# A fused recurrent tower on one core: TensorE's order rearranged, the recurrence in two blocks, half-height first scores, masks by chunk

## The chip, the cores and the metric

The program runs on one core of one Trainium2 chip. The metric is the device time of one execution in microseconds, median of the runs shown. The core's engines are TensorE (PE), VectorE (DVE), ScalarE (ACT), GpSimd (POOL) and SyncE (SP, which issues DMAs here).

## The reference, cut to what matters

```python
# x: 64 sequences of 128 token ids; table rows (50257 x 256) are quantised by tier
h   = take(quantised_table, x)                     # 64 x 128 x 256
# a layer norm, then block_forward; in its mixer, per sequence and head (8 heads of 64, 16 states):
def step((z, y), (dt, B, C, u)):
    z = (z + dt * (u*B - A*y)) / (1 + dt*dt*A)
    y = y + dt * z
    out = einsum('hpn,n->hp', y, C)
yout = (ys + D_skip * u) * silu(zgate)
x = x + yout @ out_proj.T                          # then an MLP: 256 -> 1024 -> gelu -> 256
# at last a layer norm and an int8-weight linear layer with a residual
```

The step is linear in (z, y), with a 2 x 2 matrix that depends on the head, the state and the time, but not on u. The kernel therefore computes products of these matrices along time, turns them into "keys" and "queries", and gets the outputs of 64 steps at once, as masked scores (keys times queries) times u.

## The kernel before

The program has three parts. Part one streams the embedding table to find its tier maxima and gathers the rows (0 to about 178 us). Part two is a pipeline of turns over 16 groups of 4 sequences (512 tokens a group). Part three quantises the result and multiplies by the int8 weights (the last 55 us or so). The change lies in part two.

In turn g every engine works on three groups: `first` (group g: projections, convolution, the recurrence), `second` (p = g-1: keys, queries, scores, scan output, gate, output projection) and `third` (m = g-2: the MLP and the statistics of the last norm). There are 18 turns, 0 to 17; turns 2 to 15 have all three. Each engine's order within a turn is written out by hand in `pe_turn`, `act_turn`, `dve_turn` and `pool_turn`, and semaphores join them. An engine runs its list strictly in order.

PE's list in a full turn is: `pe_z` of tiles 0 and 1 (p), transposes of the rows of g (L591), `pe_z` 2 and 3 (each waits for DVE's convolution of its tile), `pe_mlp_T` (L1030, waits for ACT's scaled rows, which wait for DVE's `dve_rms`), `pe_small` (L614), then the MLP of m: fc1 tile n (L1048) and fc2 tile n-3 (L1067), interleaved for n = 0 to 10. `pe_u_T` (L888) of p turns u back to tokens, two of four before the last two fc2 tiles, two behind. Then for each half of the heads, hg = 0 and 1: `pe_scores` (L927), a wait for DVE's masks, `pe_scan_out` (L952) in two pairs. Then `pe_u` (L604, four tiles) and `pe_out` (L973).

DVE's list is: quantise, small convolution, `dve_d` (L667), `dve_keys` (L770 to L812, waits for ACT's squares L756), `dve_layer_norm` (L907), `dve_inverse` (L815), `dve_queries`, `dve_h2`, four masks, the statistics of m, skip and gate of tiles 0 and 1, four masks, the statistics of group g+1 (L541), skip and gate of tiles 2 and 3, `dve_mean3` (L1104), `dve_bc`, the convolution of u in three portions (L851) with `dve_rms_rows` and `dve_x2` (L981) between, `dve_rms` (12 tiny dependent operations on 128x4, L997 to L1013), `dve_bk` (L733, two) and `dve_max3`.

POOL's list is: `pool_residual` (two operations on 128x1024, L1077 and L1081), 32 steps of the recurrence, `pool_norm_factors` of g+1 (waits for DVE's statistics), `pool_rstd3` (L1112 and L1114; it waits for `dve_mean3`), 32 more steps. A step is a multiplication (L747) and an addition (L749), each on 128x32 elements (2 rows of 16 lanes), and each waits for the one before. A lane stands for one chunk of 64 tokens of one sequence and head half, so 64 steps cover all. The next turn's squares on ACT (L756) need all of them.

Score matmuls have 128 keys for both chunks (ch = 0, 1) of a sequence. For chunk 0 the keys 64 to 127 are masked away by `causal`. Each mask (L938) reads a whole PSUM bank, 128x512. Scores use the banks `sbk` and `tb`; `sbk` is also where fc2 accumulates.

Of the kernel before, what the change touches and what calls it, by code (L numbers as in the profile page):

```python
# [26 lines left out]
ACT = mybir.ActivationFunctionType  # L27
# [20 lines left out]
CL = LEN // CH  # L48
SC = G * CH
# [36 lines left out]
def build(nc, a, out):  # L86
    with ExitStack() as ctx:
# [335 lines left out]
        Gs = sb("Gs", [P, CL + 1, 2, LANES])  # L423
        stp = sb("stp", [P, 2, LANES])
# [53 lines left out]
        rec = signal("rec", 2 * CL)  # L478
# [15 lines left out]
        m_ready = signal("m_ready", HG * 4)  # L494
# [241 lines left out]
        def pool_recurrence(pool, g, steps):  # L736

            if steps[0] == 0:
                if since(g):

                    pool.wait_ge(kq.sem, kq.at(g - 1))
                    pool.wait_ge(k_ready.sem, k_ready.at(g - 1))
                pool.wait_ge(x_ready.sem, x_ready.at(g))
            for t in steps:
                if t:
                    pool.wait_ge(rec.sem, rec.at(g, 2 * t))
                pool.tensor_tensor(stp[:], Gs[:, t, ::-1, :], X2[:, t, :, :], ALU.mult).then_inc(rec.sem, 1)  # L747
                pool.wait_ge(rec.sem, rec.at(g, 2 * t + 1))
                pool.tensor_tensor(Gs[:, t + 1, :, :], Gs[:, t, :, :], stp[:], ALU.add).then_inc(rec.sem, 1)  # L749

        def act_squares(act, g):
# [4 lines left out]
            act.activation(sq.rearrange("p (t a l) -> p t a l", t=CL, a=2), Gs[:, 1:, :, :], ACT.Square, scale=DOWN40) \  # L756
                .then_inc(sq_ready.sem, 1)

        def first(ap):

            return ap.rearrange("p t (s c) -> p c s t", c=CH)[:, 0]

        def second(ap):
            return ap.rearrange("p t (s c) -> p c s t", c=CH)[:, 1]

        def dve_keys(dve, g):
# [8 lines left out]
            dve.tensor_tensor(Kf[:, :, 0:CL], first(bk[:]), first(Gs[:, 0:CL, 1, :]), ALU.mult).then_inc(k_ready.sem, 1)  # L775
            dve.tensor_tensor(Kf[:, :, 2 * CL:3 * CL], second(bk[:]), second(Gs[:, 0:CL, 1, :]), ALU.mult) \
# [28 lines left out]
            t1 = sq[:, 0:2 * SC * CL].rearrange("p (a s t) -> p a s t", a=2, s=SC)  # L805
            bcast = lambda i: ends[:, i, :].unsqueeze(2).to_broadcast([P, SC, CL])
            dve.tensor_tensor(t1[:, 0], first(Gs[:, 0:CL, 1, :]), bcast(2), ALU.mult).then_inc(kq.sem, 1)
            dve.tensor_tensor(t1[:, 1], first(Gs[:, 0:CL, 0, :]), bcast(3), ALU.mult).then_inc(kq.sem, 1)
# [3 lines left out]
            dve.tensor_tensor(Kf[:, :, CL:2 * CL], first(bk[:]), t1[:, 0], ALU.mult).then_inc(k_ready.sem, 1)  # L812
# [12 lines left out]
        def pe_u(pe, g):  # L825
            for f in range(UT):
# [104 lines left out]
        def dve_mask(dve, g, hg, hh):  # L931
# [4 lines left out]
            elif since(g):  # L936
                dve.wait_ge(y_mm.sem, y_mm.at(g - 1))
            dve.tensor_tensor(MT[hh][:], score_bank[hh][:, :].rearrange("p (j t) -> p j t", j=G),  # L938
                              causal[:].rearrange("p c t -> p (c t)").unsqueeze(1).to_broadcast([P, G, LEN]),
                              ALU.mult).then_inc(m_ready.sem, 1)  # L940

        def pe_scan_out(pe, g, hg, pair):
            if hg == 0 and pair == 0:

                pe.wait_ge(z_ready.sem, z_ready.at(g))
                if since(g):
                    pe.wait_ge(gelu.sem, gelu.at(g - 1))
            pe.wait_ge(m_ready.sem, m_ready.at(g, 4 * hg + 2 * pair + 2))
# [193 lines left out]
        def pe_turn(pe):  # L1142
            def turn(g, first, second, third, nxt):
# [504 lines left out]
```

## Time and profile before

| | us |
|---|---|
| median of 3 runs | 1468.62 |
| lowest to highest | 1467.59 to 1469.27 |
| the profiled execution's own time | 1464.07 |
| its span, first to last instruction | 1462.2 |
| PE matmul busy | 1184.4 |
| DVE busy | 1160.4 |
| POOL busy | 819.6 |
| ACT busy | 757.9 |

Busy times are sums over the whole span. The span contains a streaming part in which PE does little, so they don't tell what limits a turn; for that the timeline of one turn must be read. The granted clock of TensorE has two levels here, 1.00 (2.4 GHz) and 0.50 (1.2 GHz); its mean is 0.915.

### The profile page before, as it was taken

To read this page: it belongs to the slowest core of one execution; us is meant where nothing else is said; L and a number is where in the kernel's file an instruction comes from. 1 tells how busy PE (TensorE), PEld (TensorE's weight loads), DVE (VectorE), ACT (ScalarE), POOL (GpSimd) and SP (SyncE) were. 2 spreads that over 40 slices of the span, in tenths; PEclk is the share of its full clock that TensorE was granted. 3 is DMA by queue.
4 is the path that set the end of the run, shared out by engine and by line. 5 is a ranking of instruction groups with operands and counts; after the bars stand their busy time and mean duration, and the time that the engine had idled before them with its cause. 6 is when DMAs were issued, how large, how long until landed. Compare 5 with 4: busy or idle time off the path is not lost. (4 is left out here: it accounts for less than half of the span.)

```text
span 1462.2 us, 25531 instructions
## 1 busy us (share of the span) xinstructions
PE 1184.4 (81%) x7199; PEld 814.6 (56%) x7206; DVE 1160.4 (79%) x2087; ACT 757.9 (52%) x1108; POOL 819.6 (56%) x2326
## 2 busy tenths in 40 slices
PE   0694043498989898989898989899999999898767
PEld 0352021357575756676767666666666675757444
DVE  4899933678888889888888989888888978878268
ACT  4667352354637373828273737473736555451247
POOL 7860027574757566575757575757575757560100
PEclk9999996599989899989899989998989989999889
DMA  9999400000001010101000000000000000000015
GB/s 367 408 407 425 160 23 16 12 19 16 23 10 31 1 32 3 30 6 26 10 22 16 16 16 16 16 16 16 16 16 16 16 16 16 18 17 1 0 42 188
DMA packets 62068, 92.22 MB, mean 63 GB/s; under 512 B 9101, under 2 KB 55010, under 8 KB 57554
## 3 DMA queue, kind: packets, MB, share of 16 engines
q1 hardware_dynamic: 58386, 82.10, 15.8%
q0 software_dynamic: 3072, 8.39, 1.5%
q10 hardware_dynamic: 576, 1.31, 0.2%
q8 instruction: 16, 0.26, 0.1%
q14 instruction: 18, 0.15, 0.0%
HBM read 81.29 MB, written 10.49 MB: 63 GB/s over the span
## 5 line engine op out<-in xcount | busy, mean ns | idle before, releaser
L747 POOL TENSOR_TENSOR stp<-Gs,X 128x32 f32<-128x32 f32 x1024 | 290.4, 284 | 263.1 <-ACT X L722 152.9
L749 POOL TENSOR_TENSOR Gs<-Gs,stp 128x32 f32<-128x32 f32 x1024 | 286.6, 280 | 80.3
L1048 PE MATMUL bank<-mT,w_fc 128*128 128x512 f32 x512 | 236.3, 599 | 7.9 <-ACT mT L1036 7.9
L604 PE MATMUL bank<-xT,w_in 128*128 128x512 f32 x512 | 235.8, 610 | 8.0 <-DVE uT L851 8.0
L1067 PE MATMUL bank<-w_fc,gl 128*128 128x256 f32 x1024 | 236.5, 379 | 0.0
L1067 PEld LDWEIGHTS bank<-w_fc,gl 128*128 128x128 f32 x1024 | 193.4, 190 | 59.8 <-issue 37.5
L837 ACT ACTIVATE uT<-bank,cols 128x512 f32<-128x512 f32 x64 | 49.5, 778 | 276.6 <-PE bank L604 276.6
L604 PEld LDWEIGHTS bank<-xT,w_in 128*128 128x128 f32 x512 | 97.7, 196 | 117.6 <-issue 107.1
L1048 PEld LDWEIGHTS bank<-mT,w_fc 128*128 128x128 f32 x512 | 95.7, 192 | 100.1 <-issue 94.7
L952 PE MATMUL bank<-MT,utok 128*64 128x128 f32 x1024 | 112.1, 408 | 45.5 <-DVE MT L938 45.4
L851 DVE SCALAR_TENSOR_TENSOR uT<-bank,cols,uT 128x500 f32<-128x500 f32 (+1 forms) x192 | 135.1, 736 | 3.0 <-ACT uT L837 0.7
L339 DVE TENSOR_TENSOR peak<-ring,peak 128x1536 f32<-128x1536 f32 (+2 forms) x67 | 115.3, 1722 | 19.4 <-ACT ring L242 18.0
L952 PEld LDWEIGHTS bank<-MT,utok 128*64 128x64 f32 x1024 | 101.1, 219 | 50.6 <-DVE MT L938 45.7
L938 DVE TENSOR_TENSOR MT<-bank,causal 128x512 f32<-128x512 f32 x128 | 79.5, 683 | 58.4 <-PE bank L927 58.4
L1058 ACT ACTIVATE gl<-bank,cols 128x512 f32<-128x512 f32 x128 | 84.6, 684 | 74.8 <-PE bank L1067 66.1
L242 ACT ACTIVATE ring<-ring 128x3072 f32<-128x3072 f32 (+3 forms) x35 | 90.8, 2598 | 51.0 <-DMA ring<-in_table 51.0
L973 PE MATMUL bank<-w_out,sz 128*128 128x256 f32 x512 | 113.7, 380 | 0.3 <-DVE sz L964 0.3
L973 PEld LDWEIGHTS bank<-w_out,sz 128*128 128x128 f32 x512 | 97.1, 190 | 20.9 <-issue 7.5
L815 DVE RECIPROCAL rm<-rm 128x1024 f32<-128x1024 f32 x16 | 104.7, 6542 | 0.0
L927 PE MATMUL bank<-Qf,Kf 32*128 32x64 f32 x2048 | 81.4, 319 | 21.0 <-ACT utok L897 11.2
L280 PE MATMUL bank<-ts,hot 4*128 4x256 f32 x128 | 60.4, 648 | 40.1 <-ACT hot L253 39.0
L927 PEld LDWEIGHTS bank<-Qf,Kf 32*128 32x128 f32 x2048 | 76.6, 230 | 29.2 <-issue 29.2
(171 smaller groups left out, 1899.8 us busy)
## 6 DMA issues: line engine op xcount, KB each, us to landing
ring<-in_table SPq DMA_DIRECT2D x32, 1536.0 KB, 20.9
d_rep<-d_rows SPq DMA_DIRECT2D x128, 64.0 KB, 2.7
out<-res SPq DMA_DIRECT2D x16, 512.0 KB, 2.9
b_rep<-bc_rows SPq DMA_DIRECT2D x128, 32.0 KB, 1.8
c_rep<-bc_rows SPq DMA_DIRECT2D x128, 32.0 KB, 1.8
w_fc<-in_w_fc SPq DMA_DIRECT2D x2, 1024.0 KB, 8.8
w_in<-in_w_in ACTq DMA_DIRECT2D x1, 1088.0 KB, 5.2
h<-in_table,ids POOLq DMA_INDIRECT x64, 9.8
```

What stands on the lines that cost most here:

```text
L242: act.activation(ring[n % RING][0:np_, 0:nr, :], ring[n % RING][0:np_, 0:nr, :], ACT.Abs) \
L339: return dve.tensor_tensor(acc, ring[t][0:np_, r0:r0 + nr, :], acc, ALU.max)
L604: last = pe.matmul(dst, w_in[:, k, c0:c1], xT[:, k, :], start=(k == 0), stop=(k == KD - 1))
L747: pool.tensor_tensor(stp[:], Gs[:, t, ::-1, :], X2[:, t, :, :], ALU.mult).then_inc(rec.sem, 1)
L749: pool.tensor_tensor(Gs[:, t + 1, :, :], Gs[:, t, :, :], stp[:], ALU.add).then_inc(rec.sem, 1)
L815: dve.reciprocal(rm[:], rm[:]).then_inc(inverted.sem, 1)
L851: dve.scalar_tensor_tensor(acc[:, :, i:], ps[:, :, 0:LEN - i], c("u_tap", f * TAPS + TAPS - 1 - i), acc[:, :, i:], ALU.mult, ALU.add).then ...
L927: last = pe.matmul(score_bank[hh][:, t:t + CL], Kf[own, hg * G + j, ch * CL:ch * CL + P], Qf[own, hg, t:t + CL], start=True, stop=True)
L952: last = pe.matmul(pj[head // 2][64 * (head % 2):64 * (head % 2) + 64, j * LEN:(j + 1) * LEN], utok[:, j, head * HP:(head + 1) * HP], MT[h ...
L973: last = pe.matmul(sbk[n][:, (j % 2) * D:(j % 2 + 1) * D], sz[:, f, j * LEN:(j + 1) * LEN], w_out[:, f, :], start=(f == 0), stop=(f == UT ...
L1048: last = pe.matmul(pj[n % 4][:, :], w_fc1[:, k, n * P:(n + 1) * P], mT[:, k, :], start=(k == 0), stop=(k == KD - 1))
L1067: last = pe.matmul(sbk[j // 2][:, (j % 2) * D:(j % 2 + 1) * D], gl[n % LEAD][:, j * LEN:(j + 1) * LEN], w_fc2[:, n, :], start=(n == 0 and ...
```

## The change

1. **Recurrence in two blocks.** The 64 steps of a lane become two blocks of 32 (`RB = 2`, `BL = 32`) that run side by side. `Gs` gets a block dimension. Block 1 starts from a unit state. A step's operations now cover 128x64 elements, and there are 32 steps. Before them POOL writes the unit state (one operation on 128x32), and after them `pool_join` rotates and scales all 33 states of block 1 by the end of block 0: two operations on 128x1056 and two on 128x528, all on POOL. Everything that reads `Gs` gets one more dimension.
2. **PE's order.** All four `pe_u_T` and the scores of hg = 0 move into the end of the MLP loop, the scores ahead of the last fc2 tile. `pe_u` is split: tiles 0 and 1 run between the scores of hg = 1 and their scan output, tiles 2 and 3 behind it. Scores move to the banks `tb[0], tb[1], pj[2], pj[3]`, so that they need not wait for `dve_h2`.
3. **Scores and masks.** Chunk 0 multiplies by 64 keys only. The lower 64 rows of its part of `MT` are zeroed once at the start (four memsets). A mask becomes two operations, 64x256 and 128x256: 16 a turn for 8.
4. **DVE's order.** `dve_layer_norm` moves from ahead of the inverse to behind `dve_mean3`; the row statistics of g+1 move ahead of the masks; `dve_h2` goes behind the first masks; skip is split from gate; statistics and mean of m go behind the last gate; `dve_bc` goes behind the first convolution portion.

```diff
@@ the recurrence on POOL
+                pool.tensor_tensor(Gs[:, 1, 0, :, :], unit[:], unit[:], ALU.mult).then_inc(rec.sem, 1)
+            X4 = X2[:].rearrange("p (b t) a l -> p b t a l", b=RB)
             for t in steps:
-                if t:
-                    pool.wait_ge(rec.sem, rec.at(g, 2 * t))
-                pool.tensor_tensor(stp[:], Gs[:, t, ::-1, :], X2[:, t, :, :], ALU.mult).then_inc(rec.sem, 1)
                 pool.wait_ge(rec.sem, rec.at(g, 2 * t + 1))
-                pool.tensor_tensor(Gs[:, t + 1, :, :], Gs[:, t, :, :], stp[:], ALU.add).then_inc(rec.sem, 1)
+                pool.tensor_tensor(stp[:], Gs[:, :, t, ::-1, :], X4[:, :, t, :, :], ALU.mult).then_inc(rec.sem, 1)
+                pool.wait_ge(rec.sem, rec.at(g, 2 * t + 2))
+                pool.tensor_tensor(Gs[:, :, t + 1, :, :], Gs[:, :, t, :, :], stp[:], ALU.add).then_inc(rec.sem, 1)
+
+        def pool_join(pool, g):
+            n = 2 * BL + 1
+            a = Gs[:, 0, BL, 0, :].unsqueeze(1).unsqueeze(1).to_broadcast([P, BL + 1, 2, LANES])
+            b = Gs[:, 0, BL, 1, :].unsqueeze(1).unsqueeze(1).to_broadcast([P, BL + 1, 2, LANES])
+            pool.wait_ge(rec.sem, rec.at(g, n))
+            pool.tensor_tensor(turned[:], Gs[:, 1, :, ::-1, :], b, ALU.mult).then_inc(rec.sem, 1)
+            pool.wait_ge(rec.sem, rec.at(g, n + 1))
+            pool.tensor_tensor(Gs[:, 1, :, :, :], Gs[:, 1, :, :, :], a, ALU.mult).then_inc(rec.sem, 1)
+            pool.wait_ge(rec.sem, rec.at(g, n + 2))
+            pool.tensor_tensor(Gs[:, 1, :, 0, :], Gs[:, 1, :, 0, :], turned[:, :, 0, :], ALU.subtract).then_inc(rec.sem, 1)
+            pool.tensor_tensor(Gs[:, 1, :, 1, :], Gs[:, 1, :, 1, :], turned[:, :, 1, :], ALU.add).then_inc(rec.sem, 1)
@@ scores, masks, scan output
-        score_bank = (sbk[0], sbk[1], tb[0], tb[1])
+        score_bank = (tb[0], tb[1], pj[2], pj[3])
@@
+                        keys = CL * (ch + 1)
+                        last = pe.matmul(score_bank[hh][0:keys, t:t + CL],
+                                         Kf[own, hg * G + j, ch * CL:ch * CL + keys],
                                          Qf[own, hg, t:t + CL], start=True, stop=True)
@@
+            for ch in range(CH):
+                keys = CL * (ch + 1)
+                own = lambda ap: ap.rearrange("p (j c t) -> p j c t", j=G, c=CH)[0:keys, :, ch, :]
+                dve.tensor_tensor(MT[hh][0:keys, :, ch * CL:(ch + 1) * CL], own(score_bank[hh][:, :]),
+                                  causal[0:keys, ch, :].unsqueeze(1).to_broadcast([keys, G, CL]),
+                                  ALU.mult).then_inc(m_ready.sem, 1)
@@
-            pe.wait_ge(m_ready.sem, m_ready.at(g, 4 * hg + 2 * pair + 2))
+            pe.wait_ge(m_ready.sem, m_ready.at(g, 8 * hg + 2 * (4 if hg and pair else 2 * pair + 2 + hg)))
@@ PE's turn
-                    if second and n == FT + 1:
+                    if second and n == FT:
                         pe_u_T(pe, p, g if first else None, 0)
                         pe_u_T(pe, p, g if first else None, 1)
+                    if second and n == FT + 1:
+                        pe_u_T(pe, p, g if first else None, 2)
+                        pe_u_T(pe, p, g if first else None, 3)
+                    if second and n == FT + 2:
+                        pe_scores(pe, p, 0)
@@
-                    pe_u_T(pe, p, g if first else None, 2)
-                    pe_u_T(pe, p, g if first else None, 3)
-                    for hg in range(HG):
-                        pe_scores(pe, p, hg)
-                        pe_scan_out(pe, p, hg, 0)
-                        pe_scan_out(pe, p, hg, 1)
+                    pe_scan_out(pe, p, 0, 0)
+                    pe_scan_out(pe, p, 0, 1)
+                    pe_scores(pe, p, 1)
                 if first:
-                    pe_u(pe, g)
+                    pe_u(pe, g, (0, 1))
+                if second:
+                    pe_scan_out(pe, p, 1, 0)
+                    pe_scan_out(pe, p, 1, 1)
+                if first:
+                    pe_u(pe, g, (2, 3))
@@ DVE's turn
-                    dve_layer_norm(dve, p)
                     dve_inverse(dve, p)
                     dve_queries(dve, p)
-                if third:
-                    dve_h2(dve, m)
...
+                if nxt:
+                    dve_row_stats(dve, g + 1)
                 if second:
                     for hh in range(4):
                         dve_mask(dve, p, 0, hh)
                 if third:
+                    dve_h2(dve, m)
+                if second:
+                    dve_skip(dve, p, (0, 1))
+                    for hh in range(4):
+                        dve_mask(dve, p, 1, hh)
+                    dve_gate(dve, p, (0, 1))
+                    dve_skip(dve, p, (2, 3))
+                    dve_gate(dve, p, (2, 3))
+                if third:
                     for j in range(G):
                         dve_stats3(dve, m, j)
+                    dve_mean3(dve, m)
                 if second:
...
+                    dve_layer_norm(dve, p)
+                if first:
+                    dve_conv_u(dve, g, (0, 1))
                     dve_bc(dve, g)
@@ POOL's turn
-                    pool_recurrence(pool, g, range(0, CL // 2))
+                    pool_recurrence(pool, g, range(0, BL // 2))
@@
-                    pool_recurrence(pool, g, range(CL // 2, CL))
+                    pool_recurrence(pool, g, range(BL // 2, BL))
+                    pool_join(pool, g)
```

## Rows read from the trace of the kernel before

**Rows 1.** The page: busy us, share of the span and instructions.

```profile
PE 1184.4 (81%) x7199; PEld 814.6 (56%) x7206; DVE 1160.4 (79%) x2087; ACT 757.9 (52%) x1108; POOL 819.6 (56%) x2326
```

**Rows 2.** One line's instructions, L815, once in each of 16 turns.

```profile
L815 DVE RECIPROCAL rm<-rm x16: 6534/6543/6548, 272.0 to 1323.7; 128x1024 f32<-128x1024 f32 x16
```

**Rows 3.** Timeline of PE, one full turn: start, us, work, idle before and releaser.

```profile
742.22 1.09 PE L1030 MATMUL bank<-ident,xr 128*128 128x128 f32 x8
...
745.20 7.13 PE L1048 MATMUL bank<-mT,w_fc 128*128 128x512 f32 x16 [0.46 <-ACT mT L1036]
...
769.62 1.04 PE L888 MATMUL bank<-ident,uT 128*128 128x128 f32 x8
...
773.95 1.04 PE L888 MATMUL bank<-ident,uT 128*128 128x128 f32 x8
775.86 2.01 PE L927 MATMUL bank<-Qf,Kf 32*128 32x64 f32 x64 [0.88 <-ACT utok L897]
779.28 3.35 PE L952 MATMUL bank<-MT,utok 128*64 128x128 f32 x32 [1.41 <-DVE MT L938]
...
789.33 7.13 PE L604 MATMUL bank<-xT,w_in 128*128 128x512 f32 x16
```

**Rows 4.** Windows with the granted clock: a slow and a full-speed scan output.

```profile
779.00:782.40 3.40, 3.12 (x32) 3.11 (x32) 3.31 (x8) 0.00 (x0) 2.62 (x11) 0.54 0.00 0
...
926.07:928.20 2.13, 2.03 (x32) 1.70 (x32) 2.04 (x5) 0.00 (x0) 1.40 (x6) 1.00 0.00 0
```

**Rows 5.** Timeline of DVE: end of one turn's work and the next turn.

```profile
717.84 1.41 DVE L541 BATCH_NORM_STATS2 st<-h 128x6 f32 x4
...
724.23 4.11 DVE L851 SCALAR_TENSOR_TENSOR uT<-bank,cols,uT 128x508 f32<-128x508 f32 x6
...
731.24 0.88 DVE L981 SCALAR_TENSOR_TENSOR xl<-bank,off,xl 128x256 f32<-128x256 f32 x2 [1.53 <-PE bank L973]
...
737.70 0.18 DVE L997 TENSOR_SCALAR ssq<-ssq 128x4 f32<-128x4 f32 x1
...
740.38 2.17 DVE L733 SCALAR_TENSOR_TENSOR bk<-X,cols,b_rep 128x512 f32<-128x512 f32 x2
...
753.60 1.23 DVE L770 TENSOR_TENSOR rm<-utok 128x1024 f32<-128x1024 f32 x1 [2.49 <-ACT utok L756]
...
763.66 1.67 DVE L907 SCALAR_TENSOR_TENSOR xl<-h,rs,out_b 128x256 f32<-128x256 f32 x4
...
777.94 2.48 DVE L938 TENSOR_TENSOR MT<-bank,causal 128x512 f32<-128x512 f32 x4 [2.92 <-PE bank L927]
```

**Rows 6.** Timeline of POOL in the same turns.

```profile
719.78 0.20 POOL L553 TENSOR_TENSOR lnst<-mv,eps 128x4 f32<-128x4 f32 x1 [3.64 <-DVE mv L544]
...
748.07 0.25 POOL L749 TENSOR_TENSOR Gs<-Gs,stp 128x32 f32<-128x32 f32 x1
748.61 2.35 POOL L1077 TENSOR_TENSOR h<-h,xl 128x1024 f32 x1 [0.29 <-issue]
...
794.26 1.01 POOL L1114 TENSOR_TENSOR rs<-lnst,half 128x4 f32 x1 [0.17 <-POOL lnst L1112]
```

**Rows 7.** One line's instructions: DVE L667, duration min/median/max.

```profile
L667 DVE SCALAR_TENSOR_TENSOR dd<-dt,soft x16: 280/2012/2389, 198.4 to 1241.0; 128x128 f32<-128x128 f32 x16
```

**Rows 8.** Timeline of all engines in turn 16: `dve_rms` meets `pool_residual`.

```profile
1357.70 2.34 POOL L1077 TENSOR_TENSOR h<-h,xl 128x1024 f32<-128x1024 f32 x1 [5.14 <-DVE xl L981]
...
1358.20 1.87 DVE L997 TENSOR_SCALAR ssq<-ssq 128x4 f32<-128x4 f32 x1 [0.58 <-ACT gl L991]
...
1360.20 2.34 POOL L1081 TENSOR_TENSOR h<-h,fc_b 128x1024 f32<-128x1024 f32 x1 [0.16 <-issue]
1360.31 2.26 DVE L1003 TENSOR_SCALAR ssq<-ssq 128x4 int32<-128x4 int32 x1
...
1366.13 1.97 PE L1030 MATMUL bank<-ident,xr 128*128 128x128 f32 x8 [9.49 <-ACT xr L1024]
```

**Rows 9.** Timeline of ACT in turn 1: the first squares.

```profile
258.64 1.91 ACT L756 ACTIVATE utok<-Gs 128x2048 f32<-128x2048 f32 x1 [7.16 <-POOL Gs L749]
```

More of the change, by code:

```diff
@@ L773, in dve_keys @@
                 dve.wait_ge(s_mm.sem, s_mm.at(g - 1))
-            dve.tensor_tensor(Kf[:, :, 0:CL], first(bk[:]), first(Gs[:, 0:CL, 1, :]), ALU.mult).then_inc(k_ready.sem, 1)
-            dve.tensor_tensor(Kf[:, :, 2 * CL:3 * CL], second(bk[:]), second(Gs[:, 0:CL, 1, :]), ALU.mult) \
+            before = Gs[:, :, 0:BL, 1, :]
+            dve.tensor_tensor(rows_of(Kf[:, :, 0:CL]), first(bk[:]), first(before), ALU.mult).then_inc(k_ready.sem, 1)
+            dve.tensor_tensor(rows_of(Kf[:, :, 2 * CL:3 * CL]), second(bk[:]), second(before), ALU.mult) \
                 .then_inc(k_ready.sem, 1)
@@ L803, in dve_keys @@
             dve.wait_ge(kq.sem, kq.at(g, 8))
[L805 to L808, printed above, removed]
+            t1 = sq[:, 0:2 * SC * CL].rearrange("p (a s b t) -> p a s b t", a=2, s=SC, b=RB)
+            bcast = lambda i: ends[:, i, :].unsqueeze(2).unsqueeze(2).to_broadcast([P, SC, RB, BL])
+            dve.tensor_tensor(t1[:, 0], first(before), bcast(2), ALU.mult).then_inc(kq.sem, 1)
+            dve.tensor_tensor(t1[:, 1], first(Gs[:, :, 0:BL, 0, :]), bcast(3), ALU.mult).then_inc(kq.sem, 1)
             dve.wait_ge(kq.sem, kq.at(g, 10))
@@ L823, in dve_queries, with pe_u @@
                                          ALU.mult, ALU.mult).then_inc(q_ready.sem, 1)
-        def pe_u(pe, g):
-            for f in range(UT):
+        def pe_u(pe, g, tiles):
+            for f in tiles:
                 if since(g):
@@ L954, in pe_scan_out, with dve_skip @@
             last.then_inc(y_mm.sem, 1)
-        def dve_gate(dve, g, tiles):
+        def dve_skip(dve, g, tiles):
             for f in tiles:
@@ L960, in dve_gate @@
                     .then_inc(gate1.sem, 1)
+        def dve_gate(dve, g, tiles):
             for f in tiles:
@@ L967, in pe_out @@
             pe.wait_ge(m_ready.sem, m_ready.at(g))
+            if since(g):
+                pe.wait_ge(h2_ready.sem, h2_ready.at(g - 1))
             for n in range(2):
@@ L1249, in turn @@
                 if third:
+                    dve_h2(dve, m)
[7 more added lines that the diff above has]
+                if third:
                     for j in range(G):
                         dve_stats3(dve, m, j)
+                    dve_mean3(dve, m)
                 if second:
-                    dve_gate(dve, p, (0, 1))
-                    for hh in range(4):
-                        dve_mask(dve, p, 1, hh)
-                if nxt:
-                    dve_row_stats(dve, g + 1)
-                if second:
-                    dve_gate(dve, p, (2, 3))
-                if third:
-                    dve_mean3(dve, m)
-                if first:
-                    dve_bc(dve, g)
+                    dve_layer_norm(dve, p)
                 if first:
                     dve_conv_u(dve, g, (0, 1))
+                    dve_bc(dve, g)
                 if nxt:
@@ L1328, in _ @@
             def _(dve):
-                dve.tensor_copy(Gs[:, 0, 0, :], c("part0").to_broadcast([P, LANES]))
-                dve.tensor_copy(Gs[:, 0, 1, :], c("part1").to_broadcast([P, LANES]))
+                dve.tensor_copy(Gs[:, 0, 0, 0, :], c("part0").to_broadcast([P, LANES]))
+                dve.tensor_copy(Gs[:, 0, 0, 1, :], c("part1").to_broadcast([P, LANES]))
+                dve.memset(unit[:, 0, :], 1.0)
+                dve.memset(unit[:, 1, :], 0.0)
                 dve.memset(eps5[:], 1e-5)
                 dve.memset(eps6[:], 1e-6)
+                for hh in range(4):
+                    dve.memset(MT[hh][CL:, :, 0:CL], 0.0)
                 dve.memset(half[:], -0.5).then_inc(begun, 1)
```

50 lines of the change are left out of this document (25 added, 25 removed).

## The prediction

> **What bounds the kernel now.** The page gives PE 81% and DVE 79% of the span [rows 1]: neither has much room, and these are averages over three parts, so I went on to the turns. L815 runs once in each of 16 turns, 1051.7 us from first to last [rows 2]: 70.1 us a turn. In the timeline of one turn PE runs nearly gapless from the MLP (745.20) to the last projection; its holes are 0.88 us ahead of the scores and 1.41 ahead of each scan output [rows 3]. DVE waits 2.49 us for ACT's squares, 2.92 for the scores and 1.53 for the output projection [rows 5]; with small ones, about 7 of 69. So PE sets the turn and DVE follows 7 us behind. The windows add the clock: 32 scan matmuls take 3.1 us in a stretch granted 0.54, 2.03 us at 1.00 [rows 4]. The low stretch follows the scores and their wait. POOL is off the path: its last recurrence operation ends at 748.32 [rows 6], and the squares (1.91 long [rows 9]) end only as L770 starts, at 753.60, so they begin 3.4 us behind it. Only in turn 1 does ACT wait for it, 7.16 us, for the recurrence of group 0 [rows 9].
>
> **PE's side.** I count from the start of fc1, F (745.20 in [rows 3]). To 769.62 are 24.4 us with six fc2 tiles; one fc2 tile is 1.73 ((773.95 - 769.62 - 0.87)/2), two `pe_u_T` 0.87. After the change: u_T F+22.7 to 23.6, fc2 to 25.3, u_T to 26.2, fc2 to 27.9, scores (2.01) to 29.9, fc2 to 31.6. DVE's queries are ready by about F+26.2: inverse and queries now follow the keys directly, 1.6 earlier than L907 let them [rows 5]. The masks cover 256 columns each. A mask of 512 columns costs 0.62 (2.48 for four), so one of 256 costs between 0.31 and 0.62; L907, which has 256, has a pitch of 0.41 (1.67 for four) [rows 5], and is the dearer kind. I take 0.38, so eight take 3.0: F+29.95 to 33.0. Scan output pairs take 1.05 at full clock: to F+32.7 and, after the last mask, F+34.1. Scores to 36.1; `pe_u` of two tiles (half of about 7.0) to 39.6, over the second masks (to 39.2); scan output to 41.8, `pe_u` to 45.3. DVE's skip and gate of tile 3 end at G = F+43.9. The holes of 1.4 and 0.88 are gone, and the stretch is dense, so I take the clock at 1.00 there (at 0.54 it costs up to 2.2 a turn). Loading 64 keys for 128 in half the score matmuls can gain between nothing and 1.0 us of the two 2.01; nothing here shows it, I take 0, since 64 matmuls remain. The bank change costs nothing: the gelus that free `pj` end before F+24. What DVE pays is 2 x (3.0 - 2.5), about 1.1 us a turn.
>
> **DVE's side, after G.** Statistics and their aggregation take 1.94, 717.84 to 719.78 [rows 5, 6], so `dve_mean3` has the variances at G+1.9 and ends at G+2.2. `dve_layer_norm` 1.6; `dve_bc`, four operations like the shortest L667 [rows 7], 1.2; from the first convolution to `dve_rms` 13.5 less the wait of 1.53, 12.0 [rows 5]. PE's `pe_out` is ready before each `dve_x2`, so no wait covers any of it. `dve_rms` starts at G+17.0 and takes 2.6 (737.70 to 740.38 with its last gap). Behind it wait ACT's scaling and PE's `pe_mlp_T` (742.22, 1.9 later), and fc1 3.0 later still [rows 3]: the next F at G+24.5 = 68.4. PE alone would be there sooner: from the start of `pe_u` to the next F it takes 745.20 + 70.1 - 789.33 = 26.0, less 7.0 for `pe_u`, whose end is now G+1.4, so G+20.4. The moved work has made `dve_rms` the last thing to arrive. A turn would be 68.4 against 70.1: 1.7 better, if nothing else came.
>
> **POOL's side.** 32 elements take 0.25 at a pitch of 0.33; 1024 take 2.35 [rows 6]. That is 2.12 ns an element, so 64 elements take 0.32, pitch 0.40, a step 0.80 (bounds: 0.66, as now; 1.16, if an operation on 64 cost two on 32). `pool_rstd3` waits for `dve_mean3`, starts at G+2.0 and ends at G+3.4 (0.2 and 1.01 with gaps). Sixteen steps, 12.8, and 0.7 for DVE's operations that hold it up: the join starts at **G+16.9**. Its four operations are 2.4, 2.4, 1.3 and 1.3 by the same slope, with gaps 7.9: to G+24.8. `pool_residual` of the next turn follows 0.3 later, as in [rows 6], for its input is long there: two more of 2.35, to G+29.9.
>
> So six long POOL operations start just as the twelve tiny ones of `dve_rms` do. What that costs stands in turn 16 [rows 8]. `dve_rms` met `pool_residual`: L997, 0.18 when alone [rows 5], took 1.87 and ended 0.03 after L1077; L1000 slipped through the gap; L1003 took 2.26 and ended 0.03 after L1081. L667 tells the same 16 times: 0.28 at best, 2.01 in the median, beside L1077 [rows 7]. One tiny operation gets through in each gap, then the next is held for a whole POOL operation. Six held operations, with join and residual from G+16.9 to 29.9, then the six that are left at 0.21: `dve_rms` ends at **G+31.3**, 11.7 late. The Trainium skill ("SBUF — State Buffer", Who interferes with whom) calls the port pair of the two engines an exclusive lock, held for a whole instruction, and speaks so against long operations on GpSimd beside VectorE; the trace agrees in L1077 and L667. It adds that a VectorE instruction on PSUM with one SBUF input isn't held, by which the convolution (L851) would be free; this trace has no long POOL operation beside it.
>
> PE then idles over 10 us ahead of `pe_mlp_T`. In turn 16 it did so 9.49 us, and its transposes took 1.97 where they take 1.09 [rows 8, 3]: the clock was low. I add 0.3 to the way to fc1 and 0.8 to the MLP (estimates; between nothing and 3). Turn: 43.9 + 31.3 + 1.9 + 3.3 + 0.8 = **81.2**, 11.1 more than 70.1. Turns 2 to 15 have join, residual and `dve_mean3`: 14 x 11.1 = 155.
>
> **The ends.** In turn 0 the recurrence takes 64 x 0.66 and the norm factors about 5, 47; after it 32 x 0.80 + 0.3 + 7.9 + 5, 39. ACT waits for just this [rows 9]; and since the norm factors come after half a recurrence, turn 1's other work starts earlier too, so that the 8 go through. With the gaps of turn 1: -9. Turn 16: -3 for its gaps. The memsets ahead of the first quantise, at most the 0.3 of a small operation each, +1.
>
> **Sum**, on the profiled execution's 1464.1: 1464.1 + 155 - 9 - 3 + 1 = 1608. The median of the runs stands 4.5 above that execution: 1613.
>
> **Rivals.**
> (a) *The join meets only the end of `dve_rms`.* If a step costs 0.84 or more, the join starts at G+17.6 to 19.6, and only its four operations hold `dve_rms` up. 7.5 late for 11.7: turn 77, 14 x 6.9, 1555. For it: operands have one dimension more. Against: the slope is taken over a wide range and is small.
> (b) *The join comes after `dve_rms`* (step over 0.97). Then `dve_bk` and `dve_max3` are held, the next keys start late, and DVE becomes the bound: of 69 us it works 62, less 1.7 that L667 is now held, plus 1.1, plus 10 to 11.5 held, plus 1.5 of waits: 73.5, 14 x 3.4, 1506.
> (c) *Other side, faster: join and residual hold up nothing on the path*, since they fall beside operations on PSUM, or give way to tiny ones. Turn 68.4, 14 x -1.7, edges -11: 1434. It decides at 2.5 us: if less than that is held in a turn (1.7 + 11/14), the change wins. For it: the two `dve_bk` take 2.17 together beside recurrence steps, so short POOL operations hold nothing up. Against: [rows 8], where tiny ones were held in full.
>
> **How the numbers follow.** As forecast 0.5 (its own range 1575 to 1645: cold PE from nothing to 3 less what ACT hides, scan clock low, steps from 0.77); (a) 0.15; (b) 0.1; (c) 0.2; a mixture that ends level, 0.05. The range 1485 to 1645 leaves out (c) and little else. A measurement of this kernel can tell about 0.2% from no change: faster by more 0.2, within 0.03, slower 0.77.
>
> **What would show it.** Right: join operations of 2.4 and 1.3; `dve_rms` with members of over 1 us and a length of 10 or more for 2.6; PE's wait ahead of L1030 over 8 us, released by ACT's scaled rows; L815 at a pitch near 81. The holes ahead of the scan output are gone either way. Wrong: if `dve_rms` stays near 2.6 and the pitch falls below 70; the weak step is then where the join starts, which rests on a slope and on sixteen steps.

## The result, and the profile after

The changed kernel takes 1600.95 us (median of 4 runs, 1600.06 to 1601.02) against 1468.11 for the kernel before on the same chip: 1.0911 times its time, 95% interval 1.0885 to 1.0936. The forecast was 1613, with a range of 1485 to 1645. The profiled execution of the changed kernel took 1600.94 us with a span of 1599.0. Its page, first part, answers to [rows 1]:

```profile
PE 1192.5 (75%) x7199; PEld 780.3 (49%) x7206; DVE 1298.1 (81%) x2221; ACT 756.5 (47%) x1108; POOL 711.3 (44%) x1382
```

POOL does 108 us less than in [rows 1], PE 8 more, and DVE 138 more. DVE's number is the one to distrust: its new work is small, so something must have made its instructions longer.

The reciprocal, once in each of 16 turns, now L842, gives the pitch as in [rows 2]: 1195.6 us over 15 intervals, 79.7 a turn for 70.1.

```profile
L842 DVE RECIPROCAL rm<-rm x16: 6530/6542/6549, 262.4 to 1458.0; 128x1024 f32<-128x1024 f32 x16
```

The timeline of PE in one turn answers to [rows 3] (L1063 is `pe_mlp_T`, L1081 fc1, L956 scores, L981 scan output):

```profile
723.03 7.71 PE L1081 MATMUL bank<-mT,w_fc 128*128 128x512 f32 x16
...
751.60 2.68 PE L956 MATMUL bank<-Qf,Kf 32*64 32x64 f32 x64
...
756.14 2.19 PE L981 MATMUL bank<-MT,utok 128*64 128x128 f32 x32
758.26 2.68 PE L956 MATMUL bank<-Qf,Kf 32*64 32x64 f32 x64
...
764.50 1.97 PE L981 MATMUL bank<-MT,utok 128*64 128x128 f32 x32
...
800.04 1.97 PE L1063 MATMUL bank<-ident,xr 128*128 128x128 f32 x8 [12.46 <-ACT xr L1057]
...
803.81 8.28 PE L1081 MATMUL bank<-mT,w_fc 128*128 128x512 f32 x16
```

The new order does what it should: from 723.03 to 770 there is no hole, and the scan outputs take 2.19 and 1.97 where one took 3.35 in [rows 3]. Then PE stands still for 12.46 us ahead of `pe_mlp_T`. The timeline of DVE shows what it waits for. The last gate ends at 768.46; these are `dve_rms` and the `dve_bk` behind it:

```profile
785.46 2.08 DVE L1030 TENSOR_SCALAR ssq<-ssq 128x4 f32<-128x4 f32 x1
787.58 0.17 DVE L1033 TENSOR_SCALAR ssq<-ssq 128x4 int32<-128x4 int32 x1
787.78 2.26 DVE L1036 TENSOR_SCALAR ssq<-ssq 128x4 int32<-128x4 int32 x1
790.07 0.16 DVE L1041 SCALAR_TENSOR_TENSOR ssq<-ssq 128x4 f32<-128x4 f32 x1
790.27 1.16 DVE L1044 TENSOR_TENSOR ssq<-ssq 128x4 f32<-128x4 f32 x1
791.46 1.23 DVE L1046 SCALAR_TENSOR_TENSOR ssq<-ssq 128x4 f32<-128x4 f32 x1
792.72 2.26 DVE L1041 SCALAR_TENSOR_TENSOR ssq<-ssq 128x4 f32<-128x4 f32 x1
795.02 0.16 DVE L1044 TENSOR_TENSOR ssq<-ssq 128x4 f32<-128x4 f32 x1
795.22 2.28 DVE L1046 SCALAR_TENSOR_TENSOR ssq<-ssq 128x4 f32<-128x4 f32 x1
...
798.21 2.13 DVE L737 SCALAR_TENSOR_TENSOR bk<-X,cols,b_rep 128x512 f32<-128x512 f32 x2
```

And POOL at the same time, the join (L762 to L767) and the residual (L1110, L1114):

```profile
785.08 2.44 POOL L762 TENSOR_TENSOR turned<-Gs 128x1056 f32<-128x1056 f32 x1
787.60 2.41 POOL L764 TENSOR_TENSOR Gs<-Gs 128x1056 f32<-128x1056 f32 x1
790.09 1.32 POOL L766 TENSOR_TENSOR Gs<-Gs,turned 128x528 f32<-128x528 f32 x1
791.37 1.30 POOL L767 TENSOR_TENSOR Gs<-Gs,turned 128x528 f32<-128x528 f32 x1
792.63 2.33 POOL L1110 TENSOR_TENSOR h<-h,xl 128x1024 f32 x1
795.14 2.34 POOL L1114 TENSOR_TENSOR h<-h,fc_b 128x1024 f32 x1 [0.17 <-issue]
```

Read the two side by side. L1030 ends at 787.54, and L762 ends at 787.52. L1036 ends at 790.04, L764 at 790.01. Each long POOL operation has one tiny DVE operation that ends with it; where POOL leaves a gap, one more slips through in 0.16 us. Six are held, three slip through, and three follow the last POOL operation. `dve_rms` takes 12.7 us (785.46 to 798.21 with its last gap) for 2.6.

### The profile page after: what moved, and what is told of

Its sections match the earlier page's. It is cut to its first block and busy times, and to the rows that moved or that the text cites. A ratio compares the mean times of both kernels' runs of the same rounds, so it can differ in the third digit from the quotient of the medians.

```text
span 1599.0 us, 23951 instructions
## 1 busy us (share of the span) xinstructions
PE 1192.5 (75%) x7199; PEld 780.3 (49%) x7206; DVE 1298.1 (81%) x2221; ACT 756.5 (47%) x1108; POOL 711.3 (44%) x1382
## 5 line engine op out<-in xcount | busy, mean ns | idle before, releaser
L608 PE MATMUL bank<-xT,w_in 128*128 128x512 f32 x512 | 245.8, 620 | 39.1 <-DVE uT L878 39.0
L1081 PE MATMUL bank<-mT,w_fc 128*128 128x512 f32 x512 | 247.2, 622 | 1.4 <-ACT mT L1069 1.4
L1100 PE MATMUL bank<-w_fc,gl 128*128 128x256 f32 x1024 | 243.0, 381 | 0.0
L754 POOL TENSOR_TENSOR Gs<-Gs,stp 128x64 f32<-128x64 f32 x512 | 177.6, 347 | 40.1
L752 POOL TENSOR_TENSOR stp<-Gs,X 128x64 f32<-128x64 f32 x512 | 177.3, 346 | 38.9
L1063 PE MATMUL bank<-ident,xr 128*128 128x128 f32 x128 | 30.6, 418 | 181.3 <-ACT xr L1057 181.3
L1081 PEld LDWEIGHTS bank<-mT,w_fc 128*128 128x128 f32 x512 | 100.3, 202 | 100.6 <-issue 95.9
L878 DVE SCALAR_TENSOR_TENSOR uT<-bank,cols,uT 128x500 f32<-128x500 f32 (+1 forms) x192 | 134.5, 733 | 15.3 <-ACT uT L864 13.0
L971 DVE TENSOR_TENSOR MT<-bank,causal 64x256 f32<-64x256 f32 (+1 forms) x256 | 87.5, 407 | 58.7 <-PE bank L956 58.7
L1063 PEld LDWEIGHTS bank<-ident,xr 128*128 128x128 f32 x128 | 24.4, 218 | 194.1 <-ACT xr L1057 194.1
L842 DVE RECIPROCAL rm<-rm 128x1024 f32<-128x1024 f32 x16 | 104.7, 6541 | 0.0
L1057 ACT ACTIVATE xr<-xl,ssq 128x256 f32<-128x256 f32 x64 | 27.3, 496 | 158.3 <-DVE ssq L1046 158.3
```

The source lines that it names most:

```text
L608: last = pe.matmul(dst, w_in[:, k, c0:c1], xT[:, k, :], start=(k == 0), stop=(k == KD - 1))
L752: pool.tensor_tensor(stp[:], Gs[:, :, t, ::-1, :], X4[:, :, t, :, :], ALU.mult).then_inc(rec.sem, 1)
L754: pool.tensor_tensor(Gs[:, :, t + 1, :, :], Gs[:, :, t, :, :], stp[:], ALU.add).then_inc(rec.sem, 1)
L842: dve.reciprocal(rm[:], rm[:]).then_inc(inverted.sem, 1)
L878: dve.scalar_tensor_tensor(acc[:, :, i:], ps[:, :, 0:LEN - i], c("u_tap", f * TAPS + TAPS - 1 - i), acc[:, :, i:], ALU.mult, ALU.add).then ...
L971: dve.tensor_tensor(MT[hh][0:keys, :, ch * CL:(ch + 1) * CL], own(score_bank[hh][:, :]), causal[0:keys, ch, :].unsqueeze(1).to_broadcast([ ...
```

## The experiments

The pitch is that of DVE's reciprocal in the profiled execution. Ratios are against the kernel before on the same chip.

| kernel | median us | ratio, 95% interval | us a turn |
|---|---|---|---|
| changed kernel | 1600.95 | 1.0911, 1.0885 to 1.0936 | 79.7 |
| e1: one block | 1452.75 | 0.9911, 0.9894 to 0.9927 | 69.6 |
| e2: `pool_rstd3` behind the join | 1566.35 | 1.0689, 1.0667 to 1.0710 | 77.5 |
| e3: join behind `dve_rms` | 1518.02 | 1.0359, 1.0333 to 1.0384 | 74.2 |
| e4: 128 keys | 1573.29 | 1.0738, 1.0720 to 1.0756 | 77.8 |
| e5: e2, and residual behind `dve_rms` | 1499.17 | 1.0242, 1.0225 to 1.0260 | 73.2 |
| e7: one block, 128 keys | 1432.35 | 0.9780, 0.9763 to 0.9798 | 67.9 |
| e8: e7, whole masks (order alone) | 1426.20 | 0.9752, 0.9725 to 0.9780 | 67.8 |
| e9: join in short pieces | 1483.68 | 1.0127, 1.0104 to 1.0150 | 72.1 |
| e10: two blocks alone, old order | 1578.63 | 1.0769, 1.0739 to 1.0800 | 78.2 |
| e11: e9, 128 keys, whole masks | 1468.81 | 1.0028, 1.0008 to 1.0047 | 70.7 |

All but e1, e9 and e11 differ from the kernel before by more than 2%. The runs come from several chips, so where two kernels of different chips are compared below, a difference of a few us says nothing.

**e1, one block.** All of the change except the two blocks.

```diff
-RB = 2
+RB = 1
...
-                pool.tensor_tensor(Gs[:, 1, 0, :, :], unit[:], unit[:], ALU.mult).then_inc(rec.sem, 1)
...
-                    pool_join(pool, g)
```

> The changed kernel with the recurrence in one block of 64 steps again, so without the join; orders, scores and masks stay as changed. Theory (the join and the residual hold the tiny operations of dve_rms at the SBUF port that VectorE and GpSimd share): dve_rms is back at 2.6 us for 12.6, the L-line of the inverse comes every 69 to 70 us for 79.7, time 1450 to 1470. Rival (the new orders are to blame: layer norm, statistics and the convolution now stand behind the gate on VectorE): the turn stays near 80, time above 1570. Rival (TensorE's half clock behind its long wait is the cause, not the effect): also above 1550, with dve_rms at 2.6 us.

1452.75: the two blocks and their join cost 148 us, more than the whole loss, so the new orders aren't to blame. In the timeline the RMS norm is short again (all twelve between 0.16 and 0.24), and PE's wait ahead of `pe_mlp_T` is 2.45 where it was 12.46:

```profile
733.95 0.16 DVE L1029 TENSOR_SCALAR ssq<-ssq 128x4 f32<-128x4 f32 x1
...
736.61 2.20 DVE L736 SCALAR_TENSOR_TENSOR bk<-X,cols,b_rep 128x512 f32<-128x512 f32 x2
```

**e2 and e3, the join moved.** e2 starts the join earlier, by putting `pool_rstd3` behind it; e3 starts it later, by one wait.

```diff
 e2
-                if third:
-                    pool_rstd3(pool, m)
                 if first:
                     pool_recurrence(pool, g, range(BL // 2, BL))
                     pool_join(pool, g)
+                if third:
+                    pool_rstd3(pool, m)
 e3
                     pool_recurrence(pool, g, range(BL // 2, BL))
+                    if second:
+                        pool.wait_ge(rsq.sem, rsq.at(p))
                     pool_join(pool, g)
```

> The changed kernel, but pool_rstd3 comes behind the join, so that the second half of the recurrence need not wait for dve_mean3 and the join starts some 11 us earlier, about 5 us behind G. Theory: the same four long operations then meet the convolution on PSUM, which they don't hold, and the four small operations of dve_bc, which they do (about 3.6 us); the residual, if it meets dve_rms at all, holds one or two of its operations. Turn 72 to 75 for 81, time 1490 to 1530. Rival (the work on GpSimd as such is too much for the turn): no change, 1600. Rival (convolution is held too): dve_conv_u longer than 4.0 us for its six operations, and above 1550.

> The changed kernel with one wait more: the join starts only when dve_rms has ended. The same operations on GpSimd, later. Theory: dve_rms takes 2.6 us, TensorE's wait ahead of its MLP transposes falls from 12.5 to about 3 us; instead dve_bk is held by the join, twice 2.4 us, off the path unless VectorE's next turn comes too late. Turn 70 to 73, time 1460 to 1510. Rival (the amount of work on GpSimd or on VectorE is the bound, wherever it lies): about 1600.

e2 gave 1566, 36 above its range. The join now lies at 764.93 to 772.6, and there it met `dve_bc`, whose four operations take 0.27 to 0.37 in the changed kernel. The residual then met the RMS norm all the same (L1036), from e2's timeline of DVE:

```profile
766.50 1.02 DVE L679 SCALAR_TENSOR_TENSOR bcd<-nrm 128x128 f32<-128x128 f32 x1
767.56 2.46 DVE L681 TENSOR_TENSOR bcd<-bsq,bcd 128x128 f32<-128x128 f32 x1
770.05 1.35 DVE L683 SCALAR_TENSOR_TENSOR nrm<-bcd,nrm 128x128 f32<-128x128 f32 x1
771.44 1.28 DVE L685 TENSOR_TENSOR bcd<-bc,nrm 128x128 f32<-128x128 f32 x1
...
777.70 2.29 DVE L878 SCALAR_TENSOR_TENSOR uT<-bank,cols,uT 128x508 f32<-128x508 f32 x3
779.91 0.46 DVE L1030 TENSOR_SCALAR ssq<-ssq 128x4 f32<-128x4 f32 x1
...
780.61 2.27 DVE L1036 TENSOR_SCALAR ssq<-ssq 128x4 int32<-128x4 int32 x1
```

The time alone would fit the rival that the convolution is held too (above 1550). The rows don't: L878 above, three operations in 2.29 us, runs beside L1110 (777.98 to 780.33) and takes what it takes beside POOL's short steps (2.28 in the changed kernel). What the expectation had too low is the rest. It put `dve_bc` at about 3.6 us, and its four operations take 6.1 for 1.3; the RMS norm still takes 4.85 for 2.6. Together 7.1 us a turn are held, where the changed kernel holds 10.1.

e3 gave 1518, 8 us above its range. The RMS norm is unheld; the next operations of DVE pay, from e3's timeline:

```profile
756.94 6.61 DVE L737 SCALAR_TENSOR_TENSOR bk<-X,cols,b_rep 128x512 f32<-128x512 f32 x2
763.47 5.41 DVE L1156 TENSOR_SCALAR rm<-h,mu,rs 128x256 f32 x4
```

They take 2.13 and about 1.4 unheld: 8.5 us a turn for the 10.1 that the RMS norm lost, and now it is DVE's own turn that grows, not PE's wait for the scaled rows. This is rival (b), made on purpose: it was put at 73.5 us a turn and 1506, and measures 74.2 and 1518.

**e5, both.** `pool_rstd3` as in e2, and `pool_residual` waits for the end of `dve_rms`.

```diff
                 if third:
+                    pool.wait_ge(rsq.sem, rsq.at(m))
                     pool_residual(pool, m)
```

> The changed kernel with POOL's reciprocal deviation of the MLP behind the join, as in the run that took 1566.3 us, and the residual waiting for VectorE's last RMS operation. In that run the join held the four operations of VectorE between the convolutions (6.1 us instead of 1.2) and the residual still held two of the RMS norm (12 operations in 4.9 us instead of 2.5). Taking the residual away should give back 2.4 us a turn on the path, 14 x 2.4 = 34: 1533 us, range 1515 to 1550. Rival: the residual then holds the two products bk behind the RMS norm and puts off VectorE's next turn by as much as it gave, 1555 to 1580 us.

1499.17, under its range. The join moved again (741.10 to 748.7), and met the four scalings of the next group's rows, L582, 1.67 in the changed kernel; the residual met bk and the last differences. From its timeline of DVE:

```profile
740.30 5.87 DVE L582 TENSOR_SCALAR xr<-h,mv,lnst 128x256 f32 x4
746.09 0.86 DVE L1014 SCALAR_TENSOR_TENSOR xl<-bank,off,xl 128x256 f32<-128x256 f32 x2
746.88 2.28 DVE L878 SCALAR_TENSOR_TENSOR uT<-bank,cols,uT 128x508 f32<-128x508 f32 x3
...
754.52 4.32 DVE L737 SCALAR_TENSOR_TENSOR bk<-X,cols,b_rep 128x512 f32<-128x512 f32 x2
758.75 3.42 DVE L1156 TENSOR_SCALAR rm<-h,mu,rs 128x256 f32 x4
```

L1014 and L878 run beside the join's last two operations (746.10 to 748.68) and aren't longer. So the join cost least here, 4.2 us of DVE's time (4.8 in e2), where PSUM operations cover the last third of it. The residual costs 4.2 more, on bk and the last differences. Three places were tried, and in each the held operation was another, of another kind.

**e9, the join in pieces.** Same work, each operation cut into eight of 4 time steps (the last of 5).

```diff
+            cuts = [(4 * i, 4 * i + 4 + (i == 7)) for i in range(8)]
-            pool.tensor_tensor(turned[:], Gs[:, 1, :, ::-1, :], b, ALU.mult).then_inc(rec.sem, 1)
+            for lo, hi in cuts:
+                pool.tensor_tensor(turned[:, lo:hi], Gs[:, 1, lo:hi, ::-1, :], part(1, lo, hi), ALU.mult) \
+                    .then_inc(rec.sem, 1)
...
```

> The changed kernel with each of the join's four operations cut into eight of 4 time steps (32 operations, by the recurrence's 0.32 us for 64 columns and 2.44 us for 1056 some 0.48 us for the wide ones and 0.32 us for the narrow ones, 13 us in all against 7.5). If a small VectorE operation is held to the end of the one POOL operation it meets, the twelve of the RMS norm cost about 0.5 us each, some 6 us instead of 12.6: the turn gets shorter by 5 to 6.5 us, 1600 - 14 x 5.75 = 1520 us, range 1500 to 1545. Rival: what counts is how long POOL is at work beside VectorE, however its work is cut; POOL then works 5.5 us longer beside it, and the kernel takes 1590 to 1660 us.

1483.68: 117 us less than the changed kernel, and 16 below the range, though POOL works longer: the pieces take from 746.39 to 760.1, 13.7 us for 7.6. From e9's timelines, POOL's first eight pieces and DVE:

```profile
746.39 3.42 POOL L766 TENSOR_TENSOR turned<-Gs 128x128 f32<-128x128 f32 x8
...
746.77 0.16 DVE L1039 TENSOR_SCALAR ssq<-ssq 128x4 f32<-128x4 f32 x1
...
747.32 0.38 DVE L1045 TENSOR_SCALAR ssq<-ssq 128x4 int32<-128x4 int32 x1
747.74 0.38 DVE L1050 SCALAR_TENSOR_TENSOR ssq<-ssq 128x4 f32<-128x4 f32 x1
...
751.12 2.61 DVE L737 SCALAR_TENSOR_TENSOR bk<-X,cols,b_rep 128x512 f32<-128x512 f32 x2
```

The twelve take 4.35 us for 12.7. What a tiny operation pays goes by the length of the one POOL operation that it meets, 0.38 here and 2.3 there. POOL is at work throughout the twelve in both kernels, so its being busy as such doesn't count, and this is the run that tells the two readings apart. Part of the gain has another reason: the twelve are over at 751.1, so the residual, which starts at 760.10 here and held two of them in the changed kernel, meets none. The short steps of the recurrence, 0.32 each, probably hurt little for the same cause: `dve_bc` beside them takes 1.3 us, for 1.2 in the kernel before.

**e10, two blocks alone.** The kernel before, with the recurrence edit and nothing else.

> The kernel before with nothing changed but the recurrence: two blocks and the join, in the old order, with 128 keys and whole masks. In the rows of before the second half of the recurrence starts at 725.67 us and VectorE's RMS norm at 737.70 us; sixteen steps of 0.80 us would bring the join to 738.5 us, so it begins 0.8 us into the RMS norm, with some eight of its operations to come. If long POOL operations hold them: four by the join (7.5 us), two by the residual (4.9 us), less the 1.2 us that they take unheld: 11 us a turn late, 14 x 9 to 11 = 126 to 154 over the kernel before's 1464: 1590 to 1620 us, range 1560 to 1630. Rival: the loss needs the new order, which puts the RMS norm where the join is; in the old order the join lies elsewhere and the shorter recurrence gives a gain or nothing: 1440 to 1480 us.

1578.63: within its range, 11 below the 1590 to 1620 it was first put at. The loss doesn't need the new order. The join starts at 772.37, 0.95 into the RMS norm (predicted 0.8), which runs from 771.42 to 782.2; five of its operations are held where six were counted, and the residual's second operation meets bk. From its timeline of DVE:

```profile
772.35 0.16 DVE L1038 TENSOR_TENSOR ssq<-ssq 128x4 f32<-128x4 f32 x1
772.54 2.30 DVE L1040 SCALAR_TENSOR_TENSOR ssq<-ssq 128x4 f32<-128x4 f32 x1
```

**e4, 128 keys.** The changed kernel with 128 keys in every score matmul.

```diff
-                        keys = CL * (ch + 1)
+                        keys = P
                         last = pe.matmul(score_bank[hh][0:keys, t:t + CL],
```

> The changed kernel with 128 keys in every score matmul again (masks by chunk and all else as changed; the extra lower rows are not read). With 64 keys the 64 matmuls took 2.68 us for 2.01 in the trace. Theory (the narrower weights or the alternation of widths cost TensorE time, 0.65 us twice a turn, on its path from the MLP to the gate): scores back to 2.01 us, turn 1.3 shorter, time 1580 to 1585. Rival (the scores became slower by their new place or their new PSUM banks): 2.68 us and 1601 as before.

1573.29, 27.7 us less than the changed kernel and 7 below what was expected. The score groups are back at 2.01 us, so the rival (new place, new banks) falls. From fc1 to the last gate's end e4 takes 43.5 us in one turn (713.44 to 756.97) against 45.4. Of the 1.9, 2 x 0.67 are the scores; the other 0.6 is fc1, 7.13 in that turn for 7.71. Groups of instructions, of the changed kernel (by form, then both forms together) and of e4:

```profile
L956 PE MATMUL bank<-Qf,Kf 32*128 32x64 f32 x1024 | 58.8, 300 | 0.0
L956 PE MATMUL bank<-Qf,Kf 32*64 32x64 f32 x1024 | 44.7, 245 | 5.0 <-DVE Qf L849 5.0
L956 PE MATMUL bank<-Qf,Kf 32*64 32x64 f32 (+1 forms) x2048 | 87.8, 272 | 5.0 <-DVE Qf L849 5.0
```

```profile
L956 PE MATMUL bank<-Qf,Kf 32*128 32x64 f32 x2048 | 66.3, 278 | 5.0 <-DVE Qf L849 5.0
```

A single matmul with 64 keys is shorter (245 ns for 278), but its 128-key neighbour is longer (300), and the two forms together keep PE busy 87.8 us for 66.3. The single times overlap, within a form and between the two, so neither the mean of one nor the sum of the two busy times tells the cost: read the busy time of the whole group.

**e7 and e8, toward the best version.** e7 is e1 with 128 keys; e8 has whole masks again as well, so that of the change only the order and the score banks are left.

```diff
-            for ch in range(CH):
-                keys = CL * (ch + 1)
...
+            dve.tensor_tensor(MT[hh][:], score_bank[hh][:, :].rearrange("p (j t) -> p j t", j=G),
+                              causal[:].rearrange("p c t -> p (c t)").unsqueeze(1).to_broadcast([P, G, LEN]),
+                              ALU.mult).then_inc(m_ready.sem, 1)
```

> The new order with the recurrence in one block again and 128 keys in every score matmul. If the cost of the change sits in the join and in the narrower scores, both are gone here: the one-block kernel took 1452.8 us, and 128 keys took 27.7 us off the changed kernel (1600.95 to 1573.3), of which some came from the shorter wait around the end; so 1452.8 - 20 to 28 = 1425 to 1433 us, range 1420 to 1440. Rival: in the one-block kernel the scores lie in VectorE's shadow (VectorE waits only 2.2 and 1.3 us a turn for score banks), so that 1.3 us a turn off TensorE gives back at most half, 1440 to 1450 us.

> As the kernel with one block and 128 keys, and the masks written whole as in the kernel before (four of 128x512 for each half of the heads, no kept zeros): of the change only the order of TensorE, VectorE and the score banks is left. A group of whole masks takes 2.48 us in the rows of before against 2.73 of masks by chunk, so the same as with masks by chunk, or up to 0.5 us a turn (8 us) less: 1415 to 1440 us. Rival: the masks by chunk carry the gain of the one-block kernel over the kernel before (1452.8 against 1465.4), and the order gives nothing: then 1440 to 1470 us, at least 10 us above the kernel with masks by chunk on the same chip.

1432.35 and 1426.20: e8 is the fastest kernel here, 2.5% under the kernel before. Its interval overlaps that of e7, so whether the masks by chunk cost anything stays open; they surely don't carry the gain. In e8's turn PE waits 0.81 and 1.01 us for convolutions, and here:

```profile
722.40 1.14 PE L1059 MATMUL bank<-ident,xr 128*128 128x128 f32 x8 [2.46 <-ACT xr L1053]
```

**e11, pieces with e8's other edits.** e9's join, with 128 keys and whole masks.

> The changed kernel with the join in short pieces (1483.7 us), 128 keys and whole masks. Those two gave 26.5 us with one block (1452.8 to 1426.2). If they act the same here: 1457 us, range 1448 to 1466, faster than the kernel before and still 25 to 35 us above the kernel with the new order alone (1426.2), because its RMS norm stays partly held (4.35 us against 2.65), and bk and the last operations with it. Rival: with the join cut, the shorter recurrence is worth something once TensorE has been relieved, and the time comes to within 10 us of 1426.

1468.81 over ten runs, 2.8 above the range and, against the expectation, not faster than the kernel before; the two edits gave 15 us here against 26.5 with one block. Its wait ahead of `pe_mlp_T` is 4.25 us. Even with most of the hold gone, two blocks are 43 us slower than one. What is left of the hold accounts for nearly all of it: the RMS norm takes 4.3 us for 2.6, bk 2.61 for 2.13 and the last differences 1.95 for 1.4, 2.7 us a turn, and the turn is 2.9 longer than e8's.

## Why the prediction was right, point by point

**PE's side held.** Predicted: scores at F+27.9, G = F+43.9. Measured with F = 723.03: scores at F+28.6, G at 768.46 = F+45.4. 0.6 of it is fc1 at the low clock (7.71 for 7.13), which the forecast kept apart as its +0.8, and 1.3 is the scores; that is 1.9, and 0.4 came back in the scan output and behind it. **The term that was mis-sized is the 64 keys**: "can gain between nothing and 1.0 us", taken as 0, cost 0.67 each, 1.34 a turn. A loss wasn't in the bounds; I had excluded it without a row. Removing it gave back 27.7 us (e4).

**DVE's side held.** `dve_rms` was put at G+17.0 and starts at 785.46 = G+17.0.

**POOL's side held.** A step's operation takes 0.32 at a pitch of 0.40, the join starts at G+16.6 (G+16.9), and its four operations are 2.44, 2.41, 1.32 and 1.30 (2.4, 2.4, 1.3, 1.3).

**The hold held, and is shown, not only argued.** Six held operations, as counted. The end of `dve_rms` is G+29.8 instead of G+31.3. Of the 1.5, 0.9 is that the last POOL operation ends at 797.48, G+29.0 where G+29.9 was put; the rest is that three tiny ones follow it, where the sum has six. Three had slipped through gaps, which the prediction says ("one tiny operation gets through in each gap") and its sum leaves out. e1 takes the join away and the hold with it, e9 shortens the join's operations and the hold shrinks (1.7 us a turn for 10.1), e2, e3, e5 and e10 move them and the hold follows. The rule of the Trainium skill ("SBUF — State Buffer", Who interferes with whom) that a VectorE instruction on PSUM with one SBUF input isn't held had no row beside L851 in the kernel before, but another line there, which the prediction overlooked, has one. L655, the small convolution, reads a PSUM bank and one SBUF tensor; it starts at 748.40 with three operations in 1.11 us, so that two lie beside L1077 [rows 6], and none of its 48 is longer than 0.35:

```profile
L655 DVE SCALAR_TENSOR_TENSOR bc<-bank,cols,bc x48: 339/348/350, 194.6 to 1238.0; 128x127 f32<-128x127 f32 x16, 128x126 f32<-128x126 f32 x16, 128x125 f32<-128x125 f32 x16
```

e2 and e5 show it for L851, now L878: three operations in 2.29 us beside L1110, where without it they take 2.28.

**The way on.** PE waits 12.46 us (over 10 predicted), the transposes are cold at 1.97, and fc1 takes 8.28. The clock by windows of this turn, start:end, length, busy and count for each engine, granted clock, DMA share, GB/s:

```profile
790.00:800.00 10.00, 0.00 (x0) 0.00 (x0) 9.57 (x12) 1.72 (x5) 7.23 (x5) 0.62 0.00 0
800.00:814.00 14.00, 13.96 (x65) 8.31 (x66) 8.36 (x21) 12.85 (x19) 0.00 (x0) 0.78 0.11 27
```

PE did nothing while `dve_rms` was held, the granted clock fell, and the first matmuls after the wait ran at it. The long wait isn't needed for cold transposes: in e1, with waits of 0.82, 1.00 and 2.45 us ahead of them, they take 1.97 as well. But fc1 behind them takes 7.13 there, for 7.71 to 8.28 here. The turn, from 723.03 to 803.81, is 45.4 to G, 29.8 to the end of `dve_rms` and 5.6 on to the next fc1 (5.2 predicted): 80.8 us against 81.2.

**The sum.** The fifteen intervals between reciprocals (262.42 to 1458.01, before 272.05 to 1323.71) grew by 143.9 us, for fourteen of 11.1, 155. They didn't grow alike. From turn 1 to 2, for which nothing was put, it is 6.5 (76.58 for 70.06): the join starts at 295.18 there, ahead of the RMS norm, and `dve_bc` takes 6.9 us. The next thirteen grew by 10.2 each (80.6 for 70.4). The last grew by 4.7: in turn 15 the join starts at 1429.86, when nine of the twelve are through, so it holds two of them, then bk (3.20) and the last differences (6.58). Ahead of the first reciprocal 9.6 us were gained, for 9 predicted. ACT's squares of turn 1 start 8.1 us earlier than in [rows 9], and their wait is still for POOL:

```profile
250.57 1.91 ACT L774 ACTIVATE utok<-Gs 128x2048 f32<-128x2048 f32 x1 [5.92 <-POOL Gs L767]
```

Behind the last reciprocal the time grew by 2.5, where -3 and +1 were predicted; I didn't follow this. Together, 143.9 - 9.6 + 2.5 = 136.8 on a span of 1462.2 is the 1599.0 measured. So the turns were 11 us too dear and the ends 4 too cheap: 1608 against 1600.94 for the profiled execution. Part of the closeness is luck: a missing loss (the scores, 1.3 a turn) and an overcounted one (`dve_rms`, 1.5 a turn) cancel, and so do turn 1, put at nothing, and turn 15, charged in full.

**The rivals.** (a) fell: the join didn't start later. Only in turn 15, where the RMS norm starts earlier, does it meet just the end of it. (b) is what e3 makes. (c), that nothing on the path is held, fell; its number, 1434 for an unheld turn of 68.4, is nearly what the new order gives once the two other edits are gone too: e7 1432, 67.9 a turn. With 64 keys it is 1453, 69.6. The range held (a) and (b) as well, so the time alone wouldn't have told the three apart; the rows do.

**Where the intended gain went.** POOL has 108 us less work, and in the turns of the kernel before no engine waited for the recurrence but ACT in turn 1. The time that the shorter recurrence frees ends as POOL's idle time, and its price, the join, is paid by DVE. The order's gain (38 us in e8, against 1463.86 on its chip) was real and was buried.

## What to carry to other kernels

Before moving or adding work on GpSimd, list its long operations and look in the timeline at what VectorE does beside each: what counts is how long a single GpSimd operation is, and whether a chain of tiny VectorE operations that another engine waits for lies beside it. A serial chain on an engine that is off the path isn't worth shortening if that needs long operations; and if they must be there, cut them or put them beside VectorE's work on PSUM. And bound the cost of a narrower operand from both sides: fewer columns are not surely less time.

## What the runs showed that I had not expected

- Score matmuls on 32 rows that alternate between 64 and 128 keys take 2.68 us for 64, those of 128 keys alone 2.01. Why was not tried; a kernel with all the 64-key matmuls ahead of the 128-key ones would tell whether the alternation does it.
- The hold isn't confined to operations with two tensors in SBUF: L1156 and L582, one tensor in SBUF and two scalars a partition, were held as well (5.41 and 5.87 for about 1.4 and 1.67).
- It goes both ways. In e3 the join's second and third operations take 3.14 and 2.01 us beside bk, for 2.41 and 1.32. In e5 the residual's operations, 2.33 in the changed kernel, took 3.17 and 3.03 beside DVE's 512-wide ones, from its timeline of POOL:

```profile
754.68 3.17 POOL L1110 TENSOR_TENSOR h<-h,xl 128x1024 f32 x1 [4.65 <-DVE ssq L1046]
758.02 3.03 POOL L1114 TENSOR_TENSOR h<-h,fc_b 128x1024 f32 x1 [0.17 <-issue]
```
